# Group 0's pick masks: sixteen products with an identity replaced by transposing transfers and VectorE additions

## The reference

```python
inter = xf @ c1_w.T @ c2_w.T                      # (1024 tokens, 3584), rank 16
blk = inter.reshape(B * T, n_blocks, SPARSITY)    # 56 blocks of 64
idx = jnp.argmax(blk, axis=-1) + jnp.arange(0, INTER, SPARSITY)
h = jax.nn.relu(jnp.einsum('bkm,bm->bk', w1[idx], xf))
out = jnp.einsum('bk,bkm->bm', h, w2t[idx])
return x + out
```

## Time and profile before

| | |
|---|---|
| median of 3 runs | 771.0 us (770.23 to 771.32) |
| the profiled execution | 770.48 us, its span 768.6 us |
| PE busy | 762.0 us (99%) |
| VectorE busy | 613.8 us (80%) |
| GpSimd busy | 468.8 us (61%) |
| ScalarE busy | 247.3 us (32%) |
| granted TensorE clock, mean | 1.000 of full speed |

### The profile page before, as it was taken

How to read it: one execution, slowest core, us unless ns; L and a number is a source line. 1 busy time by engine, 2 the same in 40 slices (tenths; PEclk the granted TensorE clock), 3 DMA queues, 4 the chain that set the end, 5 groups by cost and what they waited for, 6 DMA issues and landing times.

```text
span 768.6 us, 11457 instructions
## 1 busy us (share of the span) xinstructions
PE 762.0 (99%) x3586; PEld 625.1 (81%) x3586; DVE 613.8 (80%) x974; ACT 247.3 (32%) x378; POOL 468.8 (61%) x306
## 2 busy tenths in 40 slices
PE   8999999999999999999999999999999999999998
PEld 8888887478888888888888888888888888888887
DVE  5888769998887878888878788787888787778864
ACT  6347668884132120303121221203031212222120
POOL 4878898779997264646547363636464563737260
PEclk9999999999999999999999999999999999999999
DMA  9536405300222221222222222212122222222114
GB/s 319 209 109 217 171 6 156 60 15 1 69 68 71 67 70 22 68 73 68 75 68 68 75 68 68 68 53 60 44 68 75 68 75 68 68 68 68 61 38 194
DMA packets 59636, 64.19 MB, mean 84 GB/s; under 512 B 41312, under 2 KB 43616, under 8 KB 59360
## 3 DMA queue, kind: packets, MB, share of 16 engines
q1 hardware_dynamic: 59328, 62.75, 26.0%
q10 hardware_dynamic: 288, 1.18, 0.4%
HBM read 50.79 MB, written 4.19 MB: 72 GB/s over the span
## 4 chain that ended last, share of the span: by engine, by line
PE 92%; DVE 4%; ACT 2%; DMA 1%; issue 1%; SPq 0%; DVEq 0%; ACTq 0%
PE bank L1911 13%; PE bank L1912 13%; PE bank L1913 13%; PE bank L1811 12%; PE bank L1812 12%; PE bank L1813 12%; PE bank L1618 4%; PE bank L1620 4%; PE bank L1619 4%; PE bank L1802 2%; DMA x<-x_in 1%; DVE x L1302 1%; PE bank L1781 1%; DVE xn L1289 1%; ACT spread L775 1%
## 5 line engine op out<-in xcount | busy, mean ns | idle before, releaser
L1911 PE MATMUL bank<-w_hi,h_hi 128*128 128x512 f32 (+1 forms) x450 | 175.5, 390 | 0.0
L1912 PE MATMUL bank<-w_lo,h_hi 128*128 128x512 f32 (+1 forms) x450 | 175.3, 390 | 0.0
L1913 PE MATMUL bank<-w_hi,h_lo 128*128 128x512 f32 (+1 forms) x450 | 174.7, 388 | 0.0
L1415 DVE TENSOR_TENSOR x<-bank,x 128x512 f32<-128x512 f32 x207 | 132.7, 683 | 48.2 <-PE bank L1913 48.2
L638 POOL TENSOR_TENSOR lo_r<-r,slot 128x512 fp32r<-128x512 f32 x54 | 70.9, 1314 | 158.0 <-ACT slot L882 158.0
L1913 PEld LDWEIGHTS bank<-w_hi,h_lo 128*128 128x128 f32 x450 | 84.5, 188 | 18.0
L1911 PEld LDWEIGHTS bank<-w_hi,h_hi 128*128 128x128 f32 x450 | 84.5, 188 | 17.3 <-POOL w_lo L643 0.3
L1912 PEld LDWEIGHTS bank<-w_lo,h_hi 128*128 128x128 f32 x450 | 84.7, 188 | 15.0
L1811 PE MATMUL bank<-xT_hi,slot 128*128 128x512 f32 x232 | 90.5, 390 | 0.0
L1812 PE MATMUL bank<-xT_lo,slot 128*128 128x512 f32 x232 | 90.3, 389 | 0.0
L946 ACT ACTIVATE h_hi<-bank 128x512 fp32r<-128x512 f32 x56 | 33.4, 600 | 118.9 <-DVE bank L1356 81.4
(11 more groups left out here) (212 smaller groups left out, 1595.0 us busy)
## 6 DMA issues: line engine op xcount, KB each, us to landing
r<-w SPq DMA_DIRECT2D x56, 256.0 KB, 3.4
w_raw<-w SPq DMA_DIRECT2D x28, 512.0 KB, 4.0
x<-x_in SPq DMA_DIRECT2D x8, 512.0 KB, 10.7
ctx_raw<-ctx_in SPq DMA_DIRECT2D x8, 512.0 KB, 3.5
xn<-ctx_in SPq DMA_DIRECT2D x8, 512.0 KB, 4.5
out<-x SPq DMA_DIRECT2D x7, 512.0 KB, 2.6
W_raw<-wqkv SPq DMA_DIRECT2D x6, 512.0 KB, 10.9
xT_raw<-xT_in SPq DMA_DIRECT2D x1, 2048.0 KB, 19.7
```

What stands on the lines that cost most here:

```text
L1415: nc.vector.tensor_tensor(x[:, t, c], bank[unit_banks(g)[p]][:, :], x[:, t, c], ALU.add).then_inc(unit_added, 1)
L1911: nc.tensor.matmul(dst, h_hi[:, j, m], w2_hi[:, j, c], start=j == 0, stop=False)
L1912: nc.tensor.matmul(dst, h_hi[:, j, m], w2_lo[:, j, c], start=False, stop=False)
L1913: last = nc.tensor.matmul(dst, h_lo[:, j, m], w2_hi[:, j, c], start=False, stop=j == GJ - 1)
```

## The change

In group 0 the masks now take the way of the other groups. `hidden_mask`, `id_b`, its building by VectorE and the big tile `pick` are gone. `pick_first(0, n)` writes to `pick_pair`, SP issues four transposing transfers `turn_mask(0, n)` ahead of the loads for group 1, and VectorE gets `mask_first(r, b)`, one addition into the bank of each block, which waits for the product (`hid_done`) and for two transfers (`mask_loaded`), and raises `first_masked`, for which ScalarE's relu now waits. `pick_first(0, 2)` and `(0, 3)` also wait, ahead of their last instruction, for the transfer that frees their half of `pick_pair`. The cuts of blocks (0,0) and (1,0) now stand behind `pick_first(0, 2)` on VectorE. The table `FIRST_BANKS` is another. SP's loads for group 1 wait for `first_masked`, where they waited for `hid_done` alone.

```diff
-FIRST_BANKS = [3, 4, 5, 1, 2, 0, 3, 4, 5, 1, 2, 0, 3, 4, 5, 1]
+FIRST_BANKS = [3, 4, 5, 0, 3, 4, 1, 2, 5, 0, 3, 2, 4, 5, 3, 1]
...
-            with sp.Fori(PLAIN - 1, NG - 2) as g:
+            for n in range(4):
+                turn_mask(0, n)
+            sp.wait_ge(first_masked, 4)
+            next_group(0, False)
+            with sp.Fori(PLAIN, NG - 2) as g:
                 next_group(g, False)
...
             def hi_h(g, r, b):
                 if isinstance(g, int) and g < PLAIN:
-                    act.wait_ge(hid_done, 4 * g + c_order(g).index((r, b)) + 1)
+                    act.wait_ge(first_masked, c_order(g).index((r, b)) + 1)
...
-                if not plain and n >= 2:
-                    dve.wait_ge(mask_loaded[n - 2], (g - PLAIN) * 16 + 16)
-                elif not plain and not (isinstance(g, int) and g == PLAIN):
-                    dve.wait_ge(mask_loaded[n + 2], (g - PLAIN) * 16)
+                if n >= 2:
+                    dve.wait_ge(mask_loaded[n - 2], g * 16 + 16)
+                elif not (isinstance(g, int) and g == 0):
+                    dve.wait_ge(mask_loaded[n + 2], g * 16)
                 nc.vector.tensor_tensor(pk, sc, first, ALU.subtract).then_inc(pick_ready, 1)
...
+            def mask_first(r, b):
+                dve.wait_ge(hid_done, FIRST_ORDER.index((r, b)) + 1)
+                for n in range(2):
+                    dve.wait_ge(mask_loaded[2 * b + n], 16)
+                dst = by_tile(bank[c_bank(0, r, b)][:, :])
+                nc.vector.tensor_tensor(dst, dst, mask_of(r, b), ALU.add).then_inc(first_masked, 1)
...
-            nc.vector.tensor_copy(id_b[:, :], id_f[:, :]).then_inc(id_b_ready, 1)
...
             pick_first(0, 1)
             lo_u(1)
+            pick_first(0, 2)
+            mask_first(0, 0)
+            mask_first(1, 0)
             lo_h(0, 0, 0)
             lo_h(0, 1, 0)
-            pick_first(0, 2)
             pick_first(0, 3)
+            mask_first(0, 1)
+            mask_first(1, 1)
             lo_h(0, 0, 1)
             lo_h(0, 1, 1)
...
-            plain_hidden(0, 0, 1, within({1: [(hidden_mask, 0, 0), (hidden_mask, 1, 0)],
-                                          5: [(score_pair, 2)], 7: [(score_pair, 3)]}))
+            plain_hidden(0, 0, 1, within({5: [(score_pair, 2)], 7: [(score_pair, 3)]}))
             plain_hidden(0, 1, 1)
-            hidden_mask(0, 0, 1)
-            hidden_mask(0, 1, 1)
             outputs(PLAIN - 1)
```

More of the change, by code:

```diff
@@ L186, in decoder_layer @@
     sums = at("sums", 144, [P, 2, GJ, NT * P], F32)
-    pick = at("pick", 196, [P, NT, GH], BF16)
     pick_pair = at("pick_pair", 196, [P, 2, 2, GH], BF16)
@@ L206, in decoder_layer @@
     id_f = small("id_f", [P, P], F32)
-    id_b = small("id_b", [P, P], BF16)
     bqk_s = small("bqk_s", [P, 2 * DC], F32)
@@ L262, in decoder_layer @@
         ident_ready = sem("ident_ready")
-        id_b_ready = sem("id_b_ready")
         order_counted = sem("order_counted")
@@ L324, in decoder_layer @@
         masked = sem("masked")
+        first_masked = sem("first_masked")
         c2_done = sem("c2_done")
@@ L728, in add_mask @@
                 for n in range(2):
-                    pool.wait_ge(mask_loaded[2 * b + n], (g - PLAIN) * 16 + 16)
+                    pool.wait_ge(mask_loaded[2 * b + n], g * 16 + 16)
                 nc.gpsimd.tensor_tensor(by_tile(dst), by_tile(part), mask_of(r, b), ALU.add).then_inc(masked, 1)
@@ L1326, in pick_first @@
             def pick_first(g, n, off=0):
-                i = n
                 sc = score_bank[n % 2][:, :].rearrange("p (b w) -> p b w", w=BLK)
-                plain = isinstance(g, int) and g < PLAIN
-                pk = pick[:, 2 * i:2 * i + 2, :] if plain else pick_pair[:, n % 2, :, :]
-                pk = pk.rearrange("p t (b w) -> p (t b) w", w=BLK)
+                pk = pick_pair[:, n % 2, :, :].rearrange("p t (b w) -> p (t b) w", w=BLK)
                 wide = [P, BANK // BLK, BLK]
@@ L1393, in make_c22 @@
                 for n in (2, 3):
-                    dve.wait_ge(mask_loaded[n], (g - PLAIN) * 16 + 16)
+                    dve.wait_ge(mask_loaded[n], g * 16 + 16)
                 nc.vector.tensor_tensor(by_tile(bank[1][:, :]), by_tile(bank[1][:, :]), mask_of(1, 1),
@@ L1814, in product @@
                 return last
[L1816 to L1823, removed]
             def hidden_bank(g, b):
@@ L1841, in plain_hidden @@
                     pe.wait_ge(A_lo_done, cuts_before(g) + i + 1)
-                    product(dst, (slot0, slot1, slot2, cut_tmp)[i], (lo_A11, lo_r12, lo_r21, lo_r22)[i], xT_block(a, b),
-                            a == 0, False, lambda k: between(H * a + k))
+                    last = product(dst, (slot0, slot1, slot2, cut_tmp)[i], (lo_A11, lo_r12, lo_r21, lo_r22)[i],
+                                   xT_block(a, b), a == 0, a == 1, lambda k: between(H * a + k))
+                last.then_inc(hid_done, 1)
             def fast_hidden(g):
@@ L1979, in _ @@
             rank_projection(1)
-            pe.wait_ge(id_b_ready, 1)
-            plain_hidden(0, 0, 1, within({1: [(hidden_mask, 0, 0), (hidden_mask, 1, 0)],
-                                          5: [(score_pair, 2)], 7: [(score_pair, 3)]}))
+            plain_hidden(0, 0, 1, within({5: [(score_pair, 2)], 7: [(score_pair, 3)]}))
             plain_hidden(0, 1, 1)
-            hidden_mask(0, 0, 1)
-            hidden_mask(0, 1, 1)
             outputs(PLAIN - 1)
```

## The result

The changed kernel takes 776.77 us (median of 6 runs, 776.63 to 778.44), the kernel before 770.9 (6 runs, 770.23 to 771.32): 1.0085 times as long, with a 95% interval from 1.0074 to 1.0095. It is slower by 5.9 us. The profiled execution took 777.7 us with a span of 775.9, 7.3 more than the span of before. It is not the median one: two of the six runs (777.7 and 778.44) have a mean granted clock of 0.995, the other four (776.63 to 776.79) have 0.996, and no trace shows one of those four.

What follows compares the result with a forecast made beforehand. The prediction took PE, busy 762.0 of 768.6 us, to bound the kernel. Removed matmuls -1.02, idle time +6.0 and low clock +2.7 made +7.7 on 770.48, so 778.2 us, with an 8-in-10 range of 774.8 to 780.

Steps and rivals of the forecast that it cites:

- VectorE's queue: Group 0's picks, mask additions and cuts, then group 1's first pick, walked in order: unit 0's addition done at about 209.8 us.
- The stop: PE at unit 4, waiting for unit 0's addition to free bank 3: idle 6.0 us, unit 4 starting 5.0 us later.
- What comes after unit 4: Group 0's later units on reused banks: none late, the 17.10 us to group 1 stay, the 5.0 us are kept.
- SP and group 1's loads: Loads wait until 204.25 instead of 199.45; POOL first wants them at 218.11, cover 13.9 us, so no cost.
- The clock: PE after its idle time at unit 4: low pace as at the start, 2.7 us lost; lower end 0.
- the likelier case: PE's idle time at unit 4 followed by a fall of the clock: 778.2 us, chance 0.52.
- The removed matmuls: Sixteen mask matmuls gone from PE in group 0: 1.02 us less, none of it given back behind group 0.
- the sum: Whole kernel: -1.02 + 6.0 + 2.7 = +7.7 us against the profiled 770.48, giving 778.2 us.
- The stop without the clock: Rival: PE stands 6 us at unit 4 but goes on at 2.4 GHz; 775.5 us, chance 0.35.
- No stop: Rival: unit 0 is added before PE asks for its bank, only the matmuls are gone; 769.5 us, chance 0.05.
- A slow turn: Rival: pick 3's transposing transfer lands in 4.4 us, not 2.4; 780.2 us; chance 0.05, shared with other late things.

Runs made afterwards that it cites:

- Experiment 7: Changed kernel with VectorE adding units 0 and 1 ahead of the second mask additions, unit 2 ahead of group 1's first pick: 772.42 us against 770.52.
- experiment 8: Changed kernel with additions of units 0 to 8 placed earlier in VectorE's queue, units 14 and 15 on banks 1 and 3: 770.41 us against 770.43.
- experiment 4: The changed kernel itself, timed once more against the kernel before: 776.67 us against 770.43.
- experiment 2: Changed kernel with the old table of banks, masks still by transfers and VectorE: 772.58 us against 770.52 for the kernel before.
- experiment 5: Changed kernel with 12 unused matmuls on PE ahead of unit 4: 776.64 us against 770.43 for the kernel before.
- experiment 3: Changed kernel with 24 unused matmuls of 512 columns on PE ahead of unit 4: 774.92 us against 770.52 for the kernel before.
- experiment 1: Kernel before with only the new table of banks, masks still made by PE: 772.24 us against 770.52.
- experiment 6: Kernel before without the sixteen mask products, group 0 getting no masks from any engine: 770.41 us against 770.43.
- experiment 9: Kernel of experiment 8 with the low part of group 0's second w2 half cut by VectorE, not GpSimd: 770.3 us against 770.96 for the kernel before.
- experiment 10: Kernel before with the same w2 cut as in experiment 9 moved from GpSimd to VectorE, masks still on PE: 770.62 us against 770.96.

## Why the prediction was right, and where its sizes were off

The time was forecast at 778.2 us with a range from 774.8 to 780; it is 776.8. The mechanism is the one forecast: a stop of PE at unit 4 behind VectorE's queue, and a low clock after it. Point by point:

- **VectorE's queue.** The walk gave 190.52 for pick 2, 194.05 for the first mask additions, 202.85 for the landing of the last turn, 209.1 for the addition of unit 0; the profile has 190.68, 194.20, 203.03 and 209.11, and the whole profiled execution is 0.2 us later already at 186.84. This queue, in which nearly nothing waits, could be walked from durations of the trace to 0.2 us.
- **The stop.** 6.0 us forecast, 5.8 in the profile, which counts from the end of unit 3's last matmul (204.11); counted as the forecast does, from where the next start would stand (203.72 + 0.23 = 203.95) to 209.91, it is also 6.0. It is released by the addition of unit 0. Experiment 7 takes it away by moving three additions, so its cause is shown and not only read off. The wait for the transfer, 2.67 us of VectorE, is part of this stop, since it stands ahead of that addition in the queue; filled with two additions it is 1.1 us long in experiment 8, which loses nothing.
- **What comes after unit 4.** No other unit waited, as forecast.
- **SP and group 1's loads.** They went out at 204.35. POOL's first use starts at 218.12, as before (218.11), with no idle time for a load.
- **The clock.** It fell, as the likelier case said. In the profiled run the low pace lasts from 209.91 to 215.2 and costs 2.6 us, against 2.7 forecast; in that of experiment 4 unit 4 starts at 209.73 and group 1 at 229.83, which makes 3.0. But the median run loses less. The eight runs of the changed kernel with a mean clock of 0.996 take 776.4 to 776.8 us, the three with 0.995 take 777.7 to 778.4, and both profiled ones are of the second kind; against the kernel filled with 24 matmuls the loss between medians is 1.75 us. For the median this term was mis-sized by 1.0 us. That it came so near in the profiled run is in part luck: that a low stretch after a stop lasts as long as that at the start had no trace behind it, and after the shorter stops of experiments 2 and 5 it was shorter. The Trainium skill (TensorE: Matmul & The Clock Gate, "Why this matters for your kernels") warns of such gaps, and these runs agree, with 1.75 us here.
- **The removed matmuls.** "Nothing behind group 0 can give anything back: PE has no waits there to give up" is the sentence that failed. They take 1.0 us of PE, but the list of PE's waits doesn't show the 0.24 us at group 1's third product, since the profile counts them as no idle time of PE, and POOL's own queue stood right behind. For the total it mattered little: behind a stop of 5.8 us PE is late for POOL's cut, so the 1.0 us did count inside the sum, and the 0.24 us came on top as a gain.
- **What is left.** From median to median the change costs 5.9 us (6.2 in experiment 4), where the sum says 7.7. The clock takes 1.0 of the difference and the third product 0.24; the other 0.3 to 0.6 us stays open.
- **The rivals.** The stop without the clock (775.5) needs a clock that stays up; experiment 3 shows what that would give, 774.9. No stop (769.5) is experiment 8, at 770.4 and not 769.5, for the reason just given. A slow turn didn't happen: the four of group 0 landed 2.4 to 2.5 us after issue.

## What to carry to other kernels

Ahead of moving work from the busiest engine to a less busy one, walk the less busy one's queue from end to end, and ask which of its late instructions frees a buffer that the busiest engine takes again; a table of buffers and the order of that queue are one decision, and each half of it alone cost 1.7 to 2.1 us here, both together 6, and the new masks and nearly the same table with the additions in a better order cost nothing. A gain on the bounding engine is only worth what the second engine allows at the next place where both meet, and that engine may be later already by less than the list of waits shows. Where a stop can't be avoided, work that nobody needs can pay: 24 matmuls, which left 0.4 us of the stop, gave back 1.75 us, and 12, which left 3.1 us, gave back nothing that the times tell. Nothing between the two was tried.

## What the runs showed of the hardware

- The granted clock fell after shorter idle times of PE than 5.8 us. A trace shows it for 2.4 us (experiment 2: 0.62, then 0.50), for 3.1 us and for 5.8 us; in the traces with 1.6 us (experiment 1) and with 2.0 us (experiment 7) it stayed at 1.00. By the mean of each run it is below 1.000 in none of nine runs of the kernel with 1.6 us, in three of eight with 2.0 us, in two of eight with 2.4 us, and in all five and eleven with 3.1 and 5.8 us. The kernel before had 1.000 in all 19 runs that were timed beside the kernels with 1.6, 2.0 and 2.4 us. In the later sets it had 0.999 in 2 of 21 and 4 of 21, and one run of experiment 6, with no such stop in its trace, had 0.998 and the longest time of its eleven (772.43 us), so a mean a little below 1.000 alone doesn't prove that a stop caused it.
- At the start of the kernel before, the first transposes come 0.223 us apart and later ones 0.119, about the ratio of 2.4 to 1.2 GHz, while the granted clock is shown as 1.00; in the middle of the kernel the shown clock and the pace agree (starts 0.43 us apart at 0.50, 0.23 at 1.00).
- VectorE and POOL held each other up. In experiment 9, VectorE's subtraction of 128x1024 float32 between buffers took 2.79 us, and 1.58 in experiment 10, where it started 1.07 later (189.66, and 188.59). Both times it ran into the end of a subtraction of POOL and into POOL's next sum, and it ended 1.1 us after that sum's start (190.24 and 190.12). That sum took 3.40 and 3.37 us, the one after it 2.40 both times, which is what each takes elsewhere. The Trainium skill (GPSIMD Engine Reference, "1. Specifications") says that GpSimd shares its SBUF interfaces with VectorE, with contention where VectorE's instruction has two SBUF inputs, as this subtraction has; these times agree, but no run here separates it from other causes.
